# An attention out projection in three f32r products instead of one f32 product, in a fused attention and convolution kernel

## The reference, cut to what matters

```python
def reference(x, cond, Wq, Wo, b):          # x (16, 512, 1024), Wq, Wo (512, 512)
    xt = x.transpose(0, 2, 1)
    qh = heads(xt @ Wq.T)                   # (16, 8, 1024, 64), queries = keys = values
    scores = qh @ qh^T / 8
    logits = (scores * cmask + (1 - cmask) * -1e30) * rmask
    ctx = softmax(logits) @ qh              # (16, 1024, 512) once the heads are joined
    x = x + (ctx @ Wo.T).transpose(0, 2, 1)     # the out projection, all in f32
    return x + causal_conv(x, cond) + b
```

## Time and profile before

| | |
|---|---|
| time, median of 3 runs | 4283.91 us (4280.56 to 4286.85) |
| the profiled execution | 4281.65 us, of which its span is 4279.9 us |
| mean granted TensorE clock | 0.993 |
| PE matmul busy | 4128.9 us (96%) |
| ACT busy | 2849.9 us (67%) |
| POOL busy | 2595.8 us (61%) |
| DVE busy | 2491.4 us (58%) |
| first scores to last scores | 41.2 to 3995.3 us |
| convolution, from its first matmul | 4051.1 us |

### The profile page before, as it was taken

The page is one execution under the profiler, slowest core; times in us unless marked ns, Lnnn a source line. Parts: engine busy times, 40 slices in busy tenths (PEclk is TensorE's granted clock), DMA queues, the critical chain, the costliest instruction groups (busy, mean ns, idle before and its releaser), DMA issues. The chain is left out here.

```text
span 4279.9 us, 56952 instructions
## 1 busy us (share of the span) xinstructions
PE 4128.9 (96%) x18688; PEld 2721.4 (64%) x18688; DVE 2491.4 (58%) x2260; ACT 2849.9 (67%) x3905; POOL 2595.8 (61%) x1044
## 2 busy tenths in 40 slices
PE   7999999999999999999999999999999999999799
PEld 4665666666566666656666665666666566666598
DVE  4664555556455655655565565656556565656576
ACT  4775767667576766757676675767667575767465
POOL 4775757667575766757576675757667575766300
PEclk8999999999999999999999999999999999999899
DMA  3323333232333333233333323333332332332488
GB/s 104 82 67 71 80 82 94 71 88 65 74 80 79 94 74 85 65 77 80 77 94 75 84 69 76 81 74 94 75 84 70 74 83 71 94 74 60 128 285 268
DMA packets 286191, 385.34 MB, mean 90 GB/s; under 512 B 148947, under 2 KB 217171, under 8 KB 285782
## 3 DMA queue, kind: packets, MB, share of 16 engines
q1 hardware_dynamic: 285910, 381.57, 34.9%
HBM read 112.28 MB, written 67.11 MB: 42 GB/s over the span
## 5 line engine op out<-in xcount | busy, mean ns | idle before, releaser
L699 POOL TENSOR_TENSOR plo<-p,phi 128x1024 fp32r<-128x1024 f32 x1024 | 2590.4, 2541 | 1404.1 <-ACT phi L629 1399.2
L743 DVE TENSOR_REDUCE mrow<-misc 128x1 f32<-128x1024 f32 x1024 | 1214.0, 1217 | 1067.5 <-PE misc L471 1067.5
L627 ACT ACTIVATE p<-sc 128x512 f32<-128x512 f32 x2048 | 1110.0, 594 | 855.2 <-PE sc L510 610.0
L523 PE MATMUL pv<-phi,val 128*128 128x512 f32 x4096 | 1192.3, 413 | 44.0 <-issue 44.0
L629 ACT ACTIVATE phi<-p 128x1024 fp32r<-128x1024 f32 x1024 | 1086.4, 1061 | 32.5
L523 PEld LDWEIGHTS pv<-phi,val 128*128 128x128 f32 x4096 | 724.1, 188 | 372.4 <-issue 226.0
L509 PE MATMUL sc<-quer,keys 128*128 128x512 f32 x2048 | 917.2, 448 | 23.5 <-issue 18.4
L510 PE MATMUL sc<-quer,keys 96*128 96x512 f32 x2048 | 808.6, 395 | 0.0
L527 PE MATMUL pv<-plo,val 128*128 128x512 f32 x2048 | 644.2, 395 | 0.7 <-POOL plo L699 0.7
L509 PEld LDWEIGHTS sc<-quer,keys 128*128 128x128 f32 x2048 | 386.7, 189 | 195.1 <-issue 75.7
L773 DVE RECIPROCAL den<-den 128x128 f32<-128x128 f32 x512 | 468.4, 935 | 50.2 <-ACT den L616 23.9
(11 more groups left out here) (67 smaller groups left out, 2647.7 us busy)
## 6 DMA issues: line engine op xcount, KB each, us to landing
keys<-hi SPq DMA_DIRECT2D x256, 256.0 KB, 3.1
quer<-mhi SPq DMA_DIRECT2D x256, 256.0 KB, 4.4
keys<-lo SPq DMA_DIRECT2D x128, 256.0 KB, 4.9
quer<-mlo SPq DMA_DIRECT2D x128, 256.0 KB, 3.8
xo<-x SPq DMA_DIRECT2D x64, 512.0 KB, 4.0
x<-xo SPq DMA_DIRECT2D x64, 512.0 KB, 5.1
xin<-x SPq DMA_DIRECT2D x16, 2048.0 KB, 13.6
out<-stage SPq DMA_DIRECT2D x64, 512.0 KB, 6.4
```

The lines of the kernel that those rows point to most:

```text
L523: pe.matmul(pv[:, half(h)], val[:, i, t, part, :], phi[:, t % NPHI, half(h)], start=(t == 0 and part == 0), stop=False)
L627: act.activation(p32[:, t % NP32, half(h)], sc[:, h, :], ACT.Exp, scale=SCALE).then_inc(s_p32, 1)
L699: pool.tensor_tensor(plo[:, t % NPLO, :], p32[:, t % NP32, :], phi[:, t % NPHI, :].bitcast(F32), ALU.subtract).then_inc(s_plo, 1)
L743: reduced = dve.tensor_reduce(mrow[:, q:q + 1], misc[:, k, :], AX.X, ALU.max)
```

## The change

The out projection is made as three f32r products: high weights by high context, low weights by high context, high weights by low context. That is 12 f32r matmuls for an item in place of 4 in f32. The weights are split once at the start, by ACT (high) and DVE (low). `normalise` writes over `ca`; ACT then rounds a pair's context to `cth` (new function `context_high`), and POOL makes `ctl` = `ca` - `cth` (`context_low`), both in step (p+1, 1, 6). In that step ACT's list is now two exponentials, `phi`, `context_high`, the copy to `val`. The eight items move, and SP issues stores of rows at other places of its list. At the end, ACT makes the high halves and DVE the low halves. Some buffers are placed elsewhere in memory.

```diff
+HIGH_AT = (1, 6)
+LOW_AT = (1, 6)
-OUT_AT = {(0, 1, 7): 0, (1, 0, 0): 1, (1, 0, 2): 2, (1, 0, 4): 3,
-          (1, 0, 6): 4, (1, 1, 0): 5, (1, 1, 2): 6, (1, 1, 4): 7}
+OUT_AT = {(1, 0, 0): 0, (1, 0, 2): 1, (1, 0, 4): 2, (1, 0, 5): 3,
+          (1, 0, 7): 4, (1, 1, 1): 5, (1, 1, 2): 6, (1, 1, 4): 7}
...
 # SP, in the batch's list
-                        if phase != "first" and (p, i) == (1, 0):
-                            store_xo(b - 1, 0)
-                            load_xo(b - 1, 2, True)
                         if phase != "first" and (p, i) == (1, 1):
-                            store_xo(b - 1, 1)
                             load_xo(b - 1, 3, True)
...
                         if i == 0 and not end:
                             operands(*next_pair(b, p))
+                        if phase != "first" and (p, i) == (1, 0):
+                            store_xo(b - 1, 0)
+                            load_xo(b - 1, 2, True)
                         if not (end and i == 1):
                             rows(nb, np_, ni)
+                        if phase != "first" and (p, i) == (1, 0):
+                            store_xo(b - 1, 1)
...
 # PE
-                for k in range(PAIRS):
-                    last = pe.matmul(out, wo[:, k, m * P:(m + 1) * P], ct[:, k, half(h)],
-                                     start=(k == 0), stop=(k == PAIRS - 1))
+                cols = slice(m * P, (m + 1) * P)
+                for n, (w, c) in enumerate(((woh, cth), (wol, cth), (woh, ctl))):
+                    for k in range(PAIRS):
+                        last = pe.matmul(out, w[:, k, cols], c[:, k, half(h)],
+                                         start=(n == 0 and k == 0), stop=(n == 2 and k == PAIRS - 1))
...
 # ACT
+            def context_high(b, p):
+                act.wait_ge(s_cnorm, pair(b, p) + 1)
+                if not (isinstance(b, int) and b == 0):
+                    act.wait_ge(s_xo, b * 2 * DT)
+                act.activation(cth[:, p, :], ca[:, p % 2, :], ACT.Copy).then_inc(s_cth, 1)
...
                             exponentials(b, p, i, t, first)
+                            if (i, t) == HIGH_AT and not (phase == "first" and p == 0):
+                                context_high(*before(b, p))
...
+                act.wait_ge(s_woh, 16)
+                act.activation(woh[:], wo32, ACT.Copy).then_inc(s_wo_high, 1)
...
 # POOL
+            def context_low(b, p):
+                pool.wait_ge(s_cth, pair(b, p) + 1)
+                pool.tensor_tensor(ctl[:, p, :], ca[:, p % 2, :], cth[:, p, :].bitcast(F32), ALU.subtract).then_inc(s_ctl, 1)
...
                             split(b, p, i, t, phase == "first" and p == 0 and i == 0)
+                            if (i, t) == LOW_AT and not (phase == "first" and p == 0):
+                                context_low(*before(b, p))
...
 # DVE
-                dve.tensor_tensor(ct[:, p, :], ca[:, p % 2, :], den[:, p % 2, :], ALU.mult).then_inc(s_cnorm, 1)
+                dve.tensor_tensor(ca[:, p % 2, :], ca[:, p % 2, :], den[:, p % 2, :], ALU.mult).then_inc(s_cnorm, 1)
...
+                dve.wait_ge(s_wo_high, 1)
+                dve.tensor_tensor(wol[:], wo32, woh[:].bitcast(F32), ALU.subtract).then_inc(s_wol, 1)
...
 # DVE, end
-                    dve.tensor_tensor(ct[:, p, half(h)], ca[:, p % 2, half(h)], den[:, p % 2, half(h)], ALU.mult).then_inc(done, 1)
+                    dve.tensor_tensor(c, c, den[:, p % 2, half(h)], ALU.mult).then_inc(s_last_norm, 1)
+                for h in range(2):
+                    dve.wait_ge(s_last_cth, h + 1)
+                    if h == 0:
+                        dve.wait_ge(s_ctl, PAIRS * B - 1)
+                    dve.tensor_tensor(ctl[:, p, half(h)], ca[:, p % 2, half(h)], cth[:, p, half(h)].bitcast(F32),
+                                      ALU.subtract).then_inc(s_last_ctl, 1)
```

More of the change, by code:

```diff
@@ L129, in __init__ @@
             self.quer = sb("quer", [P, 4, T], F32R, place)
+            self.mneg = sb("mneg", [KT, P], F32R, place)
+            self.mask8r = sb("mask8r", [KT, P], F32R, place)
         self.xin = sb("xin0", [P, SLOTS, TH], F32)
@@ L138, in __init__ @@
             self.p32 = sb("p32", [P, NP32, T], F32, place)
+            self.val = sb("val", [P, 2, KT, 2, P], F32R, place)
         with ExitStack() as place:
@@ L144, in __init__ @@
         self.brow = sb("brow", [P, T], BF16)
+        self.spare = sb("spare", [P, 3584], F32)
         self.own = sb("own", [P, CH], F32)
@@ L197, in build_attention @@
         wq = sb("wq", [P, DT, D], F32)
-        wo = sb("wo", [P, PAIRS, D], F32)
+        woh = sb("woh", [P, PAIRS, D], F32R)
+        wol = sb("wol", [P, PAIRS, D], F32R)
         ident_r = sb("ident_r", [P, P], F32R)
@@ L212, in build_attention @@
         keys, quer, keys2, quer2 = pre.keys, pre.quer, pre.keys2, pre.quer2
-        val = sb("val", [P, 2, KT, 2, P], F32R)
+        val = pre.val
         mrow = sb("mrow", [P, KT], F32)
-        mneg = sb("mneg", [KT, P], F32R)
-        mask8r = sb("mask8r", [KT, P], F32R)
+        mneg, mask8r = pre.mneg, pre.mask8r
         p32, phi, plo = pre.p32, pre.phi, pre.plo
@@ L219, in build_attention @@
         den = sb("den", [P, 2, T], F32)
-        ct = sb("ct", [P, PAIRS, T], F32)
+        cth = sb("cth", [P, PAIRS, T], F32R)
+        ctl = sb("ctl", [P, PAIRS, T], F32R)
         xo = sb("xo", [P, 2, T], F32)
+        wo32 = xo[:].rearrange("p a t -> p (a t)").rearrange("p (k e) -> p k e", e=D)
         sc = ps("sc", [P, 2, HALF])
@@ L255, in build_attention @@
         s_cnorm = sem("s_cnorm")
+        s_woh = sem("s_woh")
+        s_wo_high = sem("s_wo_high")
+        s_wol = sem("s_wol")
+        s_cth = sem("s_cth")
+        s_ctl = sem("s_ctl")
+        s_last_norm = sem("s_last_norm")
+        s_last_cth = sem("s_last_cth")
+        s_last_ctl = sem("s_last_ctl")
         s_ones = sem("s_ones")
@@ L489, in out_project @@
                 m, h = item[1] // 2, item[1] % 2
[L490 to L493, removed]
-                for k in range(PAIRS):
-                    last = pe.matmul(out, wo[:, k, m * P:(m + 1) * P], ct[:, k, half(h)],
-                                     start=(k == 0), stop=(k == PAIRS - 1))
+                if phase == "end":
+                    if item[1] < 2:
+                        pe.wait_ge(s_last_ctl, item[1] + 1)
+                elif item[1] == 0:
+                    pe.wait_ge(s_ctl, PAIRS * (prev_b + 1))
+                cols = slice(m * P, (m + 1) * P)
[3 more added lines that the diff above has]
+                                         start=(n == 0 and k == 0), stop=(n == 2 and k == PAIRS - 1))
                 last.then_inc(full, 1)
@@ L548, in start @@
                 do("start", 0, 0, "head", PHASES["start"]["head"], (0, 0, 0))
-                pe.wait_ge(s_const, 32)
+                pe.wait_ge(s_const, 16)
             def batch(phase, b):
@@ L555, in batch @@
                             first = phase == "first" and p == 0 and i == 0
+                            if phase == "first" and (p, i, t) == (1, 0, 0):
+                                pe.wait_ge(s_wol, 1)
                             scores(b, p, i, t, first)
@@ L612, in copy_context @@
                 if i == 0 and not (isinstance(b, int) and b == 0 and p < 2):
-                    act.wait_ge(s_cnorm, pair(b, p) - 1)
+                    act.wait_ge(s_ctl, pair(b, p) - 1)
                 mine, other = slice(DK * i, DK * i + DK), slice(DK - DK * i, P - DK * i)
@@ L653, in end @@
                 copy_context(B - 1, PAIRS - 1, 1)
+                p = PAIRS - 1
+                for h in range(2):
+                    act.wait_ge(s_last_norm, h + 1)
+                    act.activation(cth[:, p, half(h)], ca[:, p % 2, half(h)], ACT.Copy).then_inc(s_last_cth, 1)
             run(act, start, batch, end)
@@ L807, in start @@
                 do("start", 0, 0, "head", PHASES["start"]["head"], (0, 0, 0))
+                weights_low()
             def batch(phase, b):
@@ L860, in end @@
                 p = PAIRS - 1
-                for h, done in enumerate((s_half, s_cnorm)):
+                for h in range(2):
                     for part in range(h * KT // 2, (h + 1) * KT // 2):
@@ L864, in end @@
                     dve.wait_ge(s_rden, KT * pair(B - 1, p) + (h + 1) * KT // 2)
-                    dve.tensor_tensor(ct[:, p, half(h)], ca[:, p % 2, half(h)], den[:, p % 2, half(h)], ALU.mult).then_inc(done, 1)
+                    c = ca[:, p % 2, half(h)]
+                    dve.tensor_tensor(c, c, den[:, p % 2, half(h)], ALU.mult).then_inc(s_last_norm, 1)
+                for h in range(2):
+                    dve.wait_ge(s_last_cth, h + 1)
[3 more added lines that the diff above has]
+                                      ALU.subtract).then_inc(s_last_ctl, 1)
                 for n, item in enumerate(PHASES["end"]["out"]):
```

6 lines of the change are left out of this document (3 added, 3 removed).

## The result

| | before | after |
|---|---|---|
| median | 4283.81 us (11 runs, 4280.56 to 4286.85) | 4295.59 us (11 runs, 4294.05 to 4311.21) |
| ratio to before | | 1.0031 [1.0022, 1.0041] |
| profiled execution, its span | 4281.65, 4279.9 us | 4294.05, 4292.3 us |
| mean granted clock | 0.993 | 0.991 |
| first and last scores start | 41.19, 3994.84 | 41.88, 4000.61 |

A forecast was written before the change was run, and what follows sets the result against it. PE was taken to bound the kernel up to the last scores; -76.8 + 85.8 + 0.6 + 6 = +15.6 us on the median of 4283.91 gave 4299.5 us, range 4291 to 4308 (chance 0.52).

The forecast's parts named there:

- items: Out items on PE, 120 within steps of batches 1 to 15: each 0.64 us shorter, 76.8 us less.
- waits of 49 places: PE idle behind late exponentials at pair ends: 1.75 us at each of 49 places, 85.8 us more.
- start: Splitting the weights on ACT and DVE at the start: costs nothing.
- tail and end: Batch 15's last head and end stretch: POOL's difference, DVE's low halves, PE's half clock; 3.9 to 6.4 us more, taken 6.
- The loop's ends: Thirteen places ahead of the loop's jump back, where PE stands anyway: 0.05 us each, 0.6 us more.
- The product: An out item's 12 f32r matmuls, 0.233 us each, take 2.79 us in place of 3.43.
- What ACT gets: context_high in (p+1,1,6) waits for normalise and delays the exponentials of t = 7; PE idles 1.75 us more.
- Rival 2: The pair-end wait is real but smaller, 1.1 to 1.5 us: 4268 to 4288 us; chance 0.16.
- What POOL gets: One more difference of 2.4 us a pair; t = 7's ends 1.9 us later, hidden, at no cost.
- rival 1: normalise starts ahead of POOL's difference, so PE waits only 0.4 us a place: 4234 us; chance 0.09.
- What is moved: Out items and SP's row stores at new places: all free, the 1.26 us wait at (1,0,4) unchanged.
- rival 4: PE's clock falls behind the new gaps, half of 49 at 1.7 us each: 4341 us, fewer 4310 to 4330; chance 0.12.

The follow-up runs named there:

- products_only: The kernel before with each out item as 12 f32r matmuls, all high weights by the context rounded once, no split: 4207.96 us, 0.9821 of before.
- copy_at_7: The changed kernel with context_high and context_low one step later, at (1, 7), behind the exponentials of t = 7: 4208.71 us, 0.9824 of before.
- split_alone: The kernel before, f32 products and item places kept, plus context_high and context_low in step (1, 6), their output unread: 4343.22 us, 1.0135 of before.
- items_as_before: The changed kernel with the eight out items at the places of the kernel before: 4350.67 us, 1.0154 of before.
- copy_twice: The changed kernel with ACT's high copy made twice in the same place: 4456.43 us, 1.0401 of before.
- normalise_at_4: The changed kernel with DVE's product normalise one step earlier, at (1, 4), the copy left in place: 4289.64 us, 1.0012 of before.
- best: The changed kernel with copy and difference at (1, 7), items 2 and 3 one step later, and DVE's end reordered: 4187.47 us, 0.9773 of before.

## Why the prediction came true, point by point

**The sum.** Its terms against what the two traces and the runs give; the span grew by 12.4 us:

| term | forecast | found | from |
|---|---|---|---|
| items | -76.8 | -76.8 | products_only, 0.64 us each |
| waits of 49 places | +85.8 | +82.3 | copy_at_7, 1.68 us each |
| clock drops in the loop | 0 | about +4.3 | batches 2 and 4 |
| start | 0 | +0.7 | first scores |
| batch 0 | 0 | -2.8 | its steps, see the last point |
| clock drop of before at 3983 | 0 | -1.6 | see below |
| tail and end | +6 | +7.1 | last scores to the convolution |

The rows without the last give 6.1 us; the last scores start 5.8 us later (3994.84 to 4000.61). The loop's ends aren't in the table: a typical batch takes 249.1 us where it took 249.25, and three waits of 1.68 less 5.12 is -0.08, so nothing of their size (forecast +0.6 in all) can be told.

**The product** was right to the hundredth, since it was read from start to start of the very matmuls it is made of the earlier trace rows. One item of after:

```profile
1086.47 1.49 PE L514 MATMUL misc<-cth,woh 128*128 128x512 f32 x4
...
1087.80 1.09 PE L514 MATMUL misc<-cth,wol 128*128 128x512 f32 x4
...
1088.73 1.09 PE L514 MATMUL misc<-ctl,woh 128*128 128x512 f32 x4
...
1089.66 0.39 PE L528 MATMUL sc<-quer,keys 128*128 128x512 f32 x1
```

The second and third group and the scores behind them start 0.93 us apart, 0.233 us a matmul. The first group stands 1.33 us ahead of the second, because behind the projection in f32 its first matmul has a start 0.40 us early and 0.79 us of length in the trace, as the scores have in that place.

**What ACT gets** was right in its mechanism, and 0.07 us a place too large. The prediction's own addition, 1460.7 - 1458.89, gives 1.81 us; it took 1.75, which is 3 us nearer in the sum, and no row told it to. At the loop's ends before has waits of 1.20 to 1.63 us, where the prediction read 1.27 to 1.6; nothing hangs on it. The hand-over from DVE to ACT, for which no row stood, is 0.12 us (1156.06 to 1156.18), within my 0.05 to 0.25. The copy took 1.06 us as taken. The copy to `val` starts 0.09 us before the copy to `cth` ends, so ACT's pieces do overlap a little more than I added up: the start that I had at +1.97 us behind the old one is at +1.88. PE's 0.65 and 1.80 us behind the exponentials came back exactly (1158.41, 1159.06, 1160.21). Rival 2 named that overlap, but for a wait under 1.57; the third place is nearest with 1.61.

**What POOL gets** was hidden, as said. It stays busy until 1165.4 in the pair end above, and no wait of PE for `plo` in the loop is in the trace. The 0.23 us between the two starts stood, so rival 1 didn't happen in any of the 63 products (the shortest took 2.77 us). With the product moved out of POOL's way in three pairs of four the time is 4234.54 us, close to the rival's price of 4234; with all four moved it isn't worth that, which neither the rival nor I had seen.

**What is moved** was free, all of it. The wait ahead of the item at (1,0,4) is there in both (the total of 15 is 19.5 us, 1.3 each):

```profile
PE misc L514 <- DVE mrow L786: 19.5, 15, 1.4
```

The prediction named the item of (0,1,7) only as a thing that moves. It was more: split_alone shows that it would have covered 15 of the 49 waits, and items_as_before that with low parts it can't. Counting a place as uncovered was right for after, because the item had gone.

**The clock.** The text named drops between 62 and 3980 us as what would prove it wrong, and there are three, from 714.7, 1021.9 and 1080.0 us on, behind stands of 1.37, 1.66 and 1.43 us; that is rival 4 in 3 of 62 places. Two neighbouring stretches at the first:

```profile
711.00:714.60 3.60, 2.23 (x11) 0.90 (x10) 0.12 (x1) 3.31 (x5) 3.60 (x3) 1.00 0.68 146
714.70:718.10 3.40, 3.40 (x8) 2.29 (x9) 2.13 (x2) 1.65 (x3) 3.40 (x2) 0.51 0.00 0
```

PE was busy for 2.23 of 3.60 us in the first, and the second is at 0.51. Batches 2 and 4 take 250.5 and 252.1 us where the other passes of the loop take 249.1, so a drop costs 1.4 to 1.5 us (forecast 1.7). The run of after that took 4311.21 us has a mean clock of 0.987 against 0.990 and 0.991; more such drops would fit that, but it has no trace to count them in. Before's drop at 3983 is missing in after although PE stands 2.19 us there.

**The tail and the end.** Batch 15's last pair, POOL and PE, in answer to the earlier trace rows:

```profile
4003.87 2.39 POOL L745 TENSOR_TENSOR ctl<-ca,cth 128x1024 fp32r<-128x1024 f32 x1
...
4006.20 2.35 POOL L735 TENSOR_TENSOR plo<-p,phi 128x1024 fp32r<-128x1024 f32 x1
...
4008.61 1.22 PE L546 MATMUL pv<-plo,val 128*128 128x512 f32 x2 [2.96 <-POOL plo L735]
...
4020.82 2.05 PE L514 MATMUL misc<-cth,woh 128*128 128x512 f32 x4 [11.00 <-DVE ctl L920]
...
4021.38 2.29 DVE L885 TENSOR_TENSOR stage<-stage,own 128x2048 f32<-128x2048 f32 x1
...
4026.17 0.69 DVE L831 TENSOR_TENSOR xo<-misc,xo 128x512 f32<-128x512 f32 x1 [2.50 <-PE misc L514]
```

All three links are there. POOL's difference of the context lies among those of `p`: the last context starts 8.21 us later than before behind scores that are 5.77 later, 2.4 us more. The two low halves put off the table by another 1.9 us (10.08 - 8.21), forecast 1.5. And PE comes back from 11.00 us of idle time at half clock: the addition starts 5.35 us behind the item's start and DVE stands 2.50 us for it. That makes 6.9 us at the first addition (12.67 - 5.77) and 7.1 at the convolution, against 6.4 at the outer end of my bounds.

**Batch 0**, 2.8 us shorter, was not in the prediction. Two of its steps are shorter, (0,0,0) by 1.28 us and (2,0,4) by 1.29. In the first it is the clock: both kernels start with 30.7 us at 0.50, and these end 9.84 us behind the first scores in before (51.03) and 7.26 behind in after (49.14); 2.6 us less at half clock are 1.3 us. In the second it is who starts first, DVE's product for the staging or POOL's difference (before, then after):

```profile
173.68 9.09 POOL L699 TENSOR_TENSOR plo<-p,phi 128x1024 fp32r<-128x1024 f32 x3 [4.40 <-ACT phi L629]
173.77 3.42 DVE L726 TENSOR_TENSOR lo<-lo,hi 128x1024 fp32r<-128x1024 f32 x1
```
```profile
174.83 1.22 DVE L769 TENSOR_TENSOR lo<-lo,hi 128x1024 fp32r<-128x1024 f32 x1
175.02 6.64 POOL L735 TENSOR_TENSOR plo<-p,phi 128x1024 fp32r<-128x1024 f32 x2 [4.68 <-ACT phi L650]
```

DVE is behind in before, and PE waits 1.01 us for its maxima in that step; in after DVE is ahead, and there is no such wait. It is the flip that rival 1 named, in another place and of no use to `normalise`.

**Left open.** What decides whether a given idle time of 1.4 us is followed by half clock, 3 times in 62, was not settled, nor why the order flipped in that one step of batch 0. The 3.9 us between forecast and result are 3.5 of the smaller wait and a sum of smaller terms, most of which the prediction didn't have, in which gains and losses nearly cancel; that they do is luck.

## What to carry to other kernels

When a change makes the bound engine's work cheaper with a new step on another engine, place that step by what it waits for: here the same copy costs 82 us of waits ahead of the exponentials, and one step later, behind them, nothing that can be told (4208.71 us, against 4207.96 for the products without any split). Before moving an operation past another engine's long instruction, look at what will then stand beside that instruction, the smallest operations included. And an item that stands between two steps may be the cover of something: ask whether it can still be there once it needs a later result.

## What the runs showed of the hardware

- A cast and a `tensor_scalar` of 8 x 128 elements on DVE took 0.45 and 0.21 us alone and 2.42 and 2.44 us beside POOL's differences of 2.4 us, in each of 15 batches (2.28 and 2.30 are means with one pair that ran alone). For a product with two operands in SBUF the profile of before had shown it (1.22 to 3.25 us); that operations this small and with one input do it as well I had not expected.
- PE's clock after idle time, at idle times between the two that the trace of before showed: behind 1.3 to 1.8 us it went to 0.50 in 3 of 62 places (after), behind 2.4 to 2.5 us in 47 of 62 (copy_twice), and in each of 15 at the 3.35 to 4.90 us of normalise_at_4. It isn't set by the idle time alone: 2.52 us were followed by 0.50 in 2 of 15 places at (1,0,0) and 2.51 us in 15 of 16 at (2,0,0), both in copy_twice; and in best it fell behind 1.30 us at a loop's end and not behind 1.90 us at another (2696.5 us). The row of the 1.30 us and the clock behind it:

```profile
3181.58 0.50 PE L528 MATMUL sc<-quer,keys 128*128 128x512 f32 x1 [1.30 <-issue]
```
```profile
3183.60:3187.00 3.40, 3.40 (x8) 2.30 (x8) 2.11 (x2) 2.14 (x3) 2.66 (x3) 0.51 0.01 2
```
- The order of two starts decides who pays. With DVE's product of 128 x 1024 elements 0.09 to 0.23 us behind POOL's difference it took 3.2 to 3.4 us, 0.19 us ahead of it 1.22 us (batch 0, step (2,0,4), above).
